# Odd maxima at the start of the loop body, the folded queries behind them, odd rows normalised by ScalarE

## The reference, cut to what matters

```python
def _L0_xattn_ref(x, latents, mask, ...):           # x: context, latents: layernorm of the 64 rows
    xn = layernorm(x, ln_x_g, ln_x_b)
    ln = layernorm(latents, ln_l_g, ln_l_b)
    q = ln @ Wq
    kv = jnp.concatenate((xn, ln), axis=1) @ Wkv     # 16 heads of 64
    k, v = jnp.split(kv, 2, axis=-1)
    sim = jnp.einsum('bhid,bhjd->bhij', q * scale, k)
    sim = jnp.where(mask_full[:, None, None, :], sim, max_neg)
    attn = jax.nn.softmax(sim, axis=-1)
    out = jnp.einsum('bhij,bhjd->bhid', attn, v)     # then @ Wout and a layernorm
...
x = x + _L0_xattn_ref(ctx_1024, _layernorm(x), mask, ...)
x = x + _L0_attn_ref(_layernorm(x), ...)
x = x + _L0_ffn_ref(_layernorm(x), ...)
```

## Time and profile before

| what | us |
|---|---|
| median of 3 runs | 814.68 (813.45 to 814.83) |
| the profiled execution | 815.53 |
| its span, first to last instruction | 813.8 |
| TensorE busy | 749.8 (92%) |
| VectorE / ScalarE / GpSimd busy | 597.5 / 590.0 / 543.7 |
| granted TensorE clock, mean | 0.98 of full speed |

### The profile page before, as it was taken

How to read it: one execution, slowest core, us unless ns; L and a number is a source line. 1 busy time by engine, 2 the same in 40 slices (tenths; PEclk the granted TensorE clock), 3 DMA queues, 4 the chain that set the end, 5 groups by cost and what they waited for, 6 DMA issues and landing times.

```text
span 813.8 us, 22676 instructions
## 1 busy us (share of the span) xinstructions
PE 749.8 (92%) x7119; PEld 418.2 (51%) x7122; DVE 597.5 (73%) x1463; ACT 590.0 (73%) x1022; POOL 543.7 (67%) x712
## 2 busy tenths in 40 slices
PE   5698999999999999999999999999999999999666
PEld 3443544546555555555464555555555646455423
DVE  5877686676777777676767777776767676776677
ACT  5377777887878687878878686878787786866262
POOL 4366667676867768686868677686768686877122
PEclk9799999999999999999999999999999999999997
DMA  6302323121221202121211212021212122110001
GB/s 187 69 13 66 98 66 82 42 62 56 55 61 31 72 18 71 45 71 40 60 56 55 61 39 74 9 71 45 71 40 60 56 56 60 44 45 19 5 0 53
DMA packets 95822, 44.44 MB, mean 55 GB/s; under 512 B 66500, under 2 KB 87848, under 8 KB 95656
## 3 DMA queue, kind: packets, MB, share of 16 engines
q1 hardware_dynamic: 95728, 43.93, 19.5%
q10 hardware_dynamic: 56, 0.05, 0.0%
HBM read 24.20 MB, written 3.34 MB: 34 GB/s over the span
## 4 chain that ended last, share of the span: by engine, by line
PE 62%; DVE 17%; issue 11%; ACT 5%; POOL 3%; DVEq 1%; DMA 1%; ACTq 0%; POOLq 0%; SPq 0%
PE bank L1472 13%; PE bank L1552 7%; PE bank L1435 6%; PE bank L1439 5%; PE bank L1437 5%; PE bank L1390 4%; DVE mx L1916 3%; PE bank L1569 3%; DVE raw L1881 3%; PE bank L1407 3%; PE bank L1366 2%; PE bank L1587 2%; DVE qkl_l L1912 2%; PE bank L1406 2%; PE bank L1624 1%
## 5 line engine op out<-in xcount | busy, mean ns | idle before, releaser
L861 POOL TENSOR_TENSOR p<-arena,p 128x512 f16<-128x512 f32 x256 | 299.4, 1173 | 126.1 <-ACT arena L1117 124.6
L1126 ACT ACTIVATE p<-bank,maskbias 128x512 f16<-128x512 f32 x224 | 155.2, 693 | 103.5 <-PE bank L1439 101.4
L1472 PE MATMUL bank<-p,xv 128*128 128x512 f16 (+1 forms) x768 | 183.0, 381 | 1.3 <-POOL p L861 0.8
L1916 DVE TENSOR_REDUCE mx<-bank 128x1 f32<-128x464 f32 x256 | 154.0, 632 | 17.8 <-PE bank L1407 16.1
L1117 ACT ACTIVATE arena<-bank,maskbias 128x512 f32<-128x512 f32 x224 | 154.8, 691 | 0.0
L1472 PEld LDWEIGHTS bank<-p,xv 128*128 128x128 f16 (+1 forms) x768 | 58.5, 97 | 69.9 <-issue 23.0
L1912 DVE TENSOR_TENSOR qkl_l<-bank,qkl_h 128x512 f16<-128x512 f32 x64 | 41.1, 686 | 68.9 <-ACT qkl_h L1106 68.8
L1435 PE MATMUL bank<-qkc_h,xtT_h 128*128 128x512 f16 (+1 forms) x256 | 86.6, 389 | 0.0
L1437 PE MATMUL bank<-qkc_l,xtT_h 128*128 128x512 f16 (+1 forms) x256 | 85.0, 379 | 0.0
L1439 PE MATMUL bank<-qkc_h,xtT_l 128*128 128x512 f16 (+1 forms) x256 | 85.0, 379 | 0.0
L1407 PE MATMUL bank<-xtT_h,qkc_h 128*128 128x400 f16 x256 | 83.3, 338 | 0.0
(11 more groups left out here) (279 smaller groups left out, 1548.4 us busy)
## 6 DMA issues: line engine op xcount, KB each, us to landing
arena<-den_dram SPq DMA_DIRECT2D x62, 128.0 KB, 3.2
qkc_h<-arena SPq DMA_DIRECT2D x30, 256.0 KB, 2.4
qkc_l<-arena SPq DMA_DIRECT2D x30, 256.0 KB, 2.5
raw<-in_ctx SPq DMA_DIRECT2D x32, 192.0 KB, 2.4
lt<-lt_dram SPq DMA_DIRECT2D x60, 32.0 KB, 2.1
arena<-in_L_xattn_Wkv SPq DMA_DIRECT2D x1, 1024.0 KB, 7.5
raw<-in_ctx SPq DMA_DIRECT2D x64, 8.0 KB, 2.0
ltT_dram<-x_all SPq DMA_DIRECT2D x4, 256.0 KB, 3.0
```

Source lines behind the costliest of these rows:

```text
L861: g.tensor_tensor(p_halves[0:r, slot, 1, :], p_all[0:r, (plan.halves_made(0, k, t) - 1) % 2, :], p_halves[0:r, slot, 0, :], ALU.subtract). ...
L1126: a.activation(p_halves[0:r, slot, 0, :], sbank[t % SRING][0:r, :], ACT.Exp, bias=bias)
L1472: op = mm(bk[:, :], halves_of[at, row, :], p_halves[at, slot, prob, :], start=tile < 2 and n == 0, stop=last and n == 2)
L1916: v.tensor_reduce(mx[:, hq_tile, part:part + 1], bk[:, 0:width], AX.X, ALU.max).then_inc(s_jobs_taken, 1)
```

## The change

The table `WINDOW` gets new steps: the odd batch's maxima go from steps 2.5 to 5 to steps 1 to 3, their transpose `MT` from 6 to 4.25; `QP` goes from 0 and 0.5 to 4.5 and 5, the first half of `QC` from 1.5 to 5.5. The mask column goes from step 7 (or 15) to 5 (or 13), `SMAX` of the self-attention from step 5 to step 6 of the body behind. The odd batches' rows are normalised by ScalarE as `x * rstd + (-mean * rstd)`; GpSimd makes the offset with two small operations. Column 127 is no longer normalised, and the mask column waits for the moments alone. A transpose `T` now waits for the rows itself.

```diff
 WINDOW = Plan(N - 400, ({0, 1, 2, 3, 4}, {0, 1, 2, 3, 4}), dict(
-    STATS={4: (0, 4)}, AGGR=4, RSTD=5, XHAT=6, MASK=7,
+    STATS={4: (0, 4)}, AGGR=4, RSTD=5, XHAT=6, MASK=5,
-    ODD=dict(T=[0], MAX=[2.5, 3, 3, 3.5, 4, 4, 4.5, 5], MT=6), AHEAD=[15.5],
-    NEXT=dict(QP=[0, 0.5], QC=[1.5, 6.5], QL=[8.5, 9.5]),
+    ODD=dict(T=[0], MAX=[1, 1, 1.5, 1.5, 2.5, 2.5, 3, 3], MT=4.25), AHEAD=[15.5],
+    NEXT=dict(QP=[4.5, 5], QC=[5.5, 6.5], QL=[8.5, 9.5]),
...
-    ... SC=17, ALIBI=[18, 20], SMAX=21, SHIFT=23, EXP=24,
+    ... SC=17, ALIBI=[18, 20], SMAX=22, SHIFT=23, EXP=24,
...
+            g.memset(minus[:, :], -1.0)
...
                 if t == at["RSTD"]:
                     pool.wait_ge(s_ctx_moments, n + 1)
                     g.tensor_tensor(ve[:, 0:CH], mv[:, 0:CH, 1], epsrow[:, 0:CH], ALU.add).then_inc(s_ctx_ve, 1)
+                    if par == 1:
+                        g.tensor_tensor(less_mean[:, 0:CH], mv[:, 0:CH, 0], minus[:, 0:CH], ALU.mult).then_inc(s_ctx_less, 1)
                     pool.wait_ge(s_ctx_ve, n + 1)
                     g.tensor_tensor(rstd[:, 0:CH], ve[:, 0:CH], nhalf[:, 0:CH], ALU.pow).then_inc(s_ctx_rstd, 1)
+                    if par == 1:
+                        pool.wait_ge(s_ctx_less, (n + 1) // 2)
+                        pool.wait_ge(s_ctx_rstd, n + 1)
+                        g.tensor_tensor(offset[:, 0:CH], less_mean[:, 0:CH], rstd[:, 0:CH], ALU.mult).then_inc(s_ctx_offset, 1)
                 if t == at["MASK"]:
-                    pool.wait_ge(s_xhat_ready, n + 1)
+                    pool.wait_ge(s_ctx_moments, n + 1)
...
+            def rows_normalised(plan, n, t):
+
+                if t == plan.at["XHAT"]:
+                    act.wait_ge(s_ctx_offset, (n + 1) // 2)
+                    for c in range(plan.CH):
+                        op = a.activation(raw[:, 1, c, 0:127], raw[:, 1, c, 0:127], ACT.Identity, scale=rstd[:, c:c + 1], bias=offset[:, c:c + 1])
+                    op.then_inc(s_xhat_ready, 1)
...
                         prep(plan, i, last, s + 0.5)
+                        if k == 1 and not last:
+                            rows_normalised(plan, b + 2, t)
...
                     if job.index == 0:
                         pe.wait_ge(s_mask_col, b + 1)
+                        pe.wait_ge(s_xhat_ready, b + 1)
...
-                if t == plan.at["XHAT"]:
+                if t == plan.at["XHAT"] and par == 0:
...
-                        op = v.tensor_scalar(raw[:, par, c, :], raw[:, par, c, :], mv[:, c, 0:1], rstd[:, c:c + 1], ALU.subtract, ALU.mult)
+                        op = v.tensor_scalar(raw[:, par, c, 0:127], raw[:, par, c, 0:127], mv[:, c, 0:1], rstd[:, c:c + 1], ALU.subtract, ALU.mult)
```

More of the change, by code:

```diff
@@ L181 @@
 WINDOW = Plan(N - 400, ({0, 1, 2, 3, 4}, {0, 1, 2, 3, 4}), dict(
-    STATS={4: (0, 4)}, AGGR=4, RSTD=5, XHAT=6, MASK=7,
+    STATS={4: (0, 4)}, AGGR=4, RSTD=5, XHAT=6, MASK=5,
     START=dict(QP=[-3, -3], QC=[-2, -2], QL=[-1, -1], T=[-2.5], MAX=[1, 1, 2, 2, 3, 3, 4, 4], MT=4.25),
-    ODD=dict(T=[0], MAX=[2.5, 3, 3, 3.5, 4, 4, 4.5, 5], MT=6), AHEAD=[15.5],
-    NEXT=dict(QP=[0, 0.5], QC=[1.5, 6.5], QL=[8.5, 9.5]),
+    ODD=dict(T=[0], MAX=[1, 1, 1.5, 1.5, 2.5, 2.5, 3, 3], MT=4.25), AHEAD=[15.5],
+    NEXT=dict(QP=[4.5, 5], QC=[5.5, 6.5], QL=[8.5, 9.5]),
     EVEN=dict(T=[7.5], MAX=[10.5, 11, 11, 11.5, 12, 12, 12.5, 13], MT=14.25), XV={2: (0, 4)},
     RDEN=(3, 7), MOVE=11, ST1=[4, 4, 6, 6], YN=[7, 7], XB=8, ST2=8, M0=9, P0=9, X1=10, X1B=20, M1=10, P1=11,
-    XH=12, XHT=13, XHT_OUT=13, QKV=14, QKV_OUT=14, VBLK=15, KEXP=15.5, SC=17, ALIBI=[18, 20], SMAX=21, SHIFT=23, EXP=24,
+    XH=12, XHT=13, XHT_OUT=13, QKV=14, QKV_OUT=14, VBLK=15, KEXP=15.5, SC=17, ALIBI=[18, 20], SMAX=22, SHIFT=23, EXP=24,
     PT=[24, 25], PT_OUT=[24, 25], PV=26, CX=27, CXT=28, CXT_OUT=28, WO=29, X2=30, P2=31.5))
@@ L229, in program @@
         s_ctx_moments = es.enter_context(nc.semaphore("ctx_moments"))
+        s_ctx_offset = es.enter_context(nc.semaphore("ctx_offset"))
+        s_ctx_less = es.enter_context(nc.semaphore("ctx_less"))
         s_ctx_rstd = es.enter_context(nc.semaphore("ctx_rstd"))
@@ L458, in program @@
         onesrow = sb("onesrow", [1, WHOLE.CH * P], F16)
+        less_mean = sb("less_mean", [P, WHOLE.CH], F32)
+        offset = sb("offset", [P, WHOLE.CH], F32)
+        minus = sb("minus", [P, WHOLE.CH], F32)
         nhalf = sb("nhalf", [P, PAIRS], F32)
@@ L1199, in attention @@
                         latents_first(0)
+                    rows_normalised(plan, 1, t)
                 def body(i, since, last):
```

## The result

The changed kernel takes 860.12 us, median of four runs (859.33 to 860.73), where the kernel before takes 814.35 (813.45 to 814.83): 1.0566 of its time, 95% interval 1.0549 to 1.0582. That is 45.8 us slower; the forecast was 850, in a range of 828 to 864, and most likely 842 to 858, which the result exceeds by 2. The profiled execution has a span of 859.0, 45.2 more than before.

The account below looks back on a forecast made before the run. TensorE's list was taken to bound the loop. Added waits of 4.0 less 1.19 gone gave 2.8 us a body, taken as 2.5, 33 us for 13; with bodies 0 and 1, 35.5, so 850 us, range 828 to 864.

Parts of the forecast that it names:

- (e): First QC behind the second QP: TensorE waits for QP to be taken out, new wait 1.5 us a body.
- (f): Second QC one step behind the first: TensorE waits until both halves are taken, new wait 1.05 us a body.
- (c): First odd maximum, early in the body: TensorE waits for the DMA of the folded queries, new wait 0.75 us.
- (a): Odd rows' transpose: its wait for the mask column goes, with ScalarE normalising and the mask earlier; gain 0.59 us a body.
- (b): Old waits for the maxima's copy, ahead of the first QC and inside the maxima go; gain 0.6 us a body.
- (d): Odd maxima in pairs run at VectorE's pace: fourth and eighth wait about 0.25 each, new wait 0.5 us a body.
- (g): VectorE in steps 6 and 7: even transpose taken late, so the first QL waits some 0.2 us.
- Only the queries' waits: Rival: DMA moves land in time and maxima absorb each other; 1.55 us a body, 836 us; chance 0.17.
- The move comes late: Rival: the reciprocal keeps its place, so the first odd maximum's DMA wait is 1.85 us; 865 us; chance 0.1.
- Faster: Rival: the copies behind QP and QC are hidden and only the gains stay; 798 us; chance 0.07.
- no change: Rival: added waits equal the gains, or something both leave alone bounds the loop; chance 0.03.

Follow-up runs that it names:

- e8: The changed kernel with QP at steps 3.5 and 4 instead of 4.5 and 5, both ahead of MT: 839.9 us, 1.0316 of the kernel before.
- e4: The changed kernel with QP back at steps 0 and 0.5 and QC at 4.5 and 6.5: 826.59 us, 1.0137 of the kernel before.
- e6: e4 with the transpose of the maxima MT at step 5.25 instead of 4.25, behind the first QC: 820.84 us, 1.0075 of the kernel before.
- e10: The changed kernel with the odd maxima half a step to a step later (1.5 to 3.5): 866.71 us, 1.064 of the kernel before.
- e1: The changed kernel with the old steps for maxima, queries and SMAX, keeping only rows on ScalarE and the early mask: 811.54 us, 0.9958 of the kernel before.
- e2: The kernel before with only the new steps for maxima, queries and SMAX; rows on VectorE, mask at step 7: 882.91 us, 1.0825.
- e12: e11 with also the last odd maximum at step 4.5 and MT at 5.25: 836.23 us, 1.0254 of the kernel before.
- e11: The kernel before with only the mask column at step 5, rows still on VectorE, the transpose waiting for the rows itself: 823.9 us, 1.0125.

## Why the prediction came out as it did

**What bounds the kernel.** Right. TensorE's list bounds the loop: the waits at its own instructions give 3.05 of the 3.18 us that a body grew. 40.4 of the 45.2 us lie in the 13 loop bodies.

**(e) and (f), the folds behind their projection.** Right in mechanism, place and size: 1.49 for 1.5, and 1.14 for 1.05, both counted as the forecast counted (1.39 and 1.03 by the values' 0.75 ahead of a `QC`). e8 prices (e) at 20 us. For (f) there is the wait itself, 12.7 over the loop, and e4 and e6 in which it is absent. ScalarE shows the reason, the copy of `QP` behind the exponentials of its step, and VectorE's take behind that:

```profile
240.56 0.69 ACT L1146 ACTIVATE p<-bank,maskbias 128x512 f16<-128x512 f32 x1 [2.06 <-PE bank L1463]
241.71 0.60 ACT L1107 ACTIVATE arena<-bank 128x512 f16<-128x512 f32 x1
244.20 1.26 ACT L1115 ACTIVATE arena<-bank,ident 128x512 f16<-128x512 f32 x2 [1.89 <-PE bank L1414]
```

```profile
242.34 0.69 DVE L1927 SCALAR_TENSOR_TENSOR arena<-bank,arena 128x512 f16<-128x512 f32 x1 [2.29 <-ACT arena L1107]
244.92 1.41 DVE L1932 SCALAR_TENSOR_TENSOR arena<-bank,ident,arena 128x512 f16<-128x512 f32 x2 [1.89 <-ACT arena L1115]
```

From the start of the exponential of step 5 (240.56) to the first `QC` (243.16) it is 2.60; the forecast had 2.62 from that point (2.89 less 0.27). From there to the second it is 3.22, where it had 3.2 to 3.3. Both engines were idle for about 2 us before they began: they were not short of time, the order kept them.

**(c), the DMA.** The number was right, 0.68 for 0.75; its standing as a cost of its own was wrong, as e10 shows: GpSimd's spread is the limit there, and the 1.22 that (c) and the keys' wait take together would stay with a DMA that lands in time (an estimate from the rows of e10). That a wait which decides nothing brought 0.75 of these 1.22 into the sum is luck. The issue (225.57) comes 0.64 behind the body's start, where I had 0.77.

**(a), the rows on ScalarE.** The gain was mis-sized and its cost overlooked. "1.15 at the overlapped price" took ScalarE's operation with one pointer operand out of PSUM as its measure. Measured:

```profile
L1125 ACT ACTIVATE raw<-raw,offset,rstd x48: 482/486/490, 174.8 to 701.3; 128x127 f32<-128x127 f32 x48
```

That is 0.49 each and 1.64 for four. The page of the Trainium skill that the prediction named, "ScalarE: Activation LUTs", section "What ACT_TABLE_LOAD costs", gives by its price an estimate of 0.48 and 1.63: the trace agrees with the page, and the nearest row was the worse guide. The transpose keeps a wait of 0.19; that is the sign of being wrong that the prediction named for a price above 1.6, and it came in small. The failed sentence is the next one: "They push the exponentials of step 15 back by some 0.5; their products are wanted in step 1 of the next body, over 2 us later, so that costs nothing." The push was 0.9, and I followed the exponentials to TensorE's values and not to GpSimd, which stands between them and has the spread of the keys queued behind. That gave 0.54 a body, 7 us: the largest single thing that the forecast lacked. e1, with the old table, has this wait as well, and e2, with the old rows, has none.

**(b), (d), (g).** Gone 0.79 for 0.6, added 0.34 for 0.5: the eighth maximum waits, the fourth does not. (g) has no wait in any body: the four chunks of even rows take 1.95 as before (246.24 and 233.87).

**The sum.** The terms gave 2.81, the trace 3.05 at the same places and 3.18 in all. From 2.81 I took 2.5, since small terms are "most easily absorbed by each other": they were not, and it cost 4 us of the 10 that the forecast was short of. The missed keys are 7. The 0.13 of a body that no place holds is 1.7, the terms that came out smaller give 3.9 back, and the first body of the loop grew by 0.9 less than the others: 4.0 + 7.0 + 1.7 - 3.9 - 0.9 = 7.9 in the loop. Outside it the forecast had 2.5 and the trace has 4.8 (3.0 in bodies 0 and 1, 0.5 ahead of them, and 1.3 behind, where the forecast had nothing), so 2.3 more: 10.2 in all. The loop's part was told by errors of both signs; that a body takes 47.75, above the 46.8 to 47.4 named as the sign of being right, is the better measure of the miss. The stretches that the earlier trace rows calls bodies 0 and 1 were counted back from the loop's period. By the starts of their scores the two are 46.56 and 46.32 long (33.13, 79.69, 126.01), with 5.8 and 3.6 us of idle TensorE and not 4.2 and 3.4. The 5 us that the forecast allowed for even rows stretched by GpSimd did not come in this kernel; in e12 that stretching did.

**Rivals.** "Only the queries' waits" needed (c) and (d) at nothing, and they were there, 0.68 and 0.34. "The move comes late" gave 865 and lies nearer to the result than the forecast, but its mechanism did not happen in this kernel: the wait is 0.68. It did happen in e2, where the rows stay on VectorE (22.3 over 13 bodies is 1.7). "Faster" and "no change" are refuted.

## What to carry to other kernels

When a producer and its consumer both stand in the list of an engine that is the bound, count the latency of the copies between them with everything queued ahead of them on the copying engines, and compare it with the work that the bound engine has in between: here 2.9 and 3.2 us against 1.3 and 2.1, and that told both waits to about a tenth of a microsecond. Follow a delayed instruction to every engine that it feeds and to what is queued behind it there, not only to its last user; and when a wait at such a place is moved or removed, look at what else arrives then, since two waits that overlap each look like a whole gain. A change made of two halves should be run in halves: here one half alone was 0.4% faster and the other 8% slower.

## What the runs showed of the hardware

That a copy of 0.19 us, moved ahead of GpSimd's long operations, goes with a result of VectorE that comes 1 us later in every body was not expected. The normalisations of the kernel before differ more than threefold (least, median and greatest duration in ns):

```profile
L1881 DVE TENSOR_SCALAR raw<-raw,mv,rstd x104: 325/334/1183, 144.5 to 705.0; 128x128 f32<-128x128 f32 x104
```

In e11 it is 324, 327 and 1305. The slow ones seen in order of time all lie beside long operations of GpSimd: its low halves, 1.16 us each, and in e12, where one lasts 1.94, line 929 with 1.91. The Trainium skill, "SBUF — State Buffer", section "SBUF: two separate sides", has VectorE and GpSimd share a port that one of them holds for its whole instruction; the trace agrees so far as that the two chunks of 2.44 us end with GpSimd's two low halves (352.01 and 351.93) and two without them take 0.58. By the same section ScalarE never waits for another engine's port, and its row operations, which run beside GpSimd's low halves too (222.53 and 221.93), keep to 482 to 490 ns in all 48 cases. e1 and e11 have the same early mask and differ in the engine of the odd rows: 811.54 against 823.9.
